# Issuing the first attention weight loads ahead of the weight-split stage, and squaring the next x tile at another place of VectorE's queue, in an attention + FFN block on eight cores

## The reference

```
xn = (x - mean) / sqrt(var + 1e-5)                    # over the 1024 features
# attention: 16 query heads, 4 kv heads, head size 64, window of 16 keys back
q = rmsnorm(xn @ wq.T); k = rmsnorm(xn @ wk.T); v = xn @ wv.T
attn = softmax(q k^T / 8 + alibi bias, masked to 0 <= i-j <= 16) @ v
a = attn @ wo.T
# FFN (RWKV channel mix); x_prev is xn shifted by one token
xr = mu_r*xn + (1-mu_r)*x_prev;  xk = mu_k*xn + (1-mu_k)*x_prev
f = sigmoid(xr @ W_r.T) * (relu(xk @ W_k.T)**2 @ W_v.T)
return x + a + f
```

## Time and profile before

| | us |
|---|---|
| median of 3 runs | 2063.03 |
| the three runs | 2060.89, 2063.03, 2120.01 |
| profiled execution, its own time | 2056.66 |
| span of its slowest core (core 5) | 2055.1 |
| spans of the eight cores | 2027.7 to 2055.1 |

### The profile page before, as it was taken

One profiled execution on the slowest core, in us unless ns is written; L12 is line 12 of the kernel. 1 busy time (PEld: TensorE's weight loads), 2 busy tenths in 40 slices (PEclk: granted clock), 3 DMA queues, 4 the chain that ended last, 5 costly groups with the idle time before them and its releaser, 6 DMA issues.

```text
span 2055.1 us, 19870 instructions; the slowest of 8 cores (2027.7 to 2055.1 us)
## 1 busy us (share of the span) xinstructions
PE 1601.4 (78%) x8032; PEld 970.7 (47%) x8032; DVE 557.7 (27%) x667; ACT 191.9 (9%) x280; POOL 273.9 (13%) x245
## 2 busy tenths in 40 slices
PE   1014987887897998789697997789699798779798
PEld 0002425885342435787242434778243343678443
DVE  1127343220013632330013723231011624332011
ACT  0000011110000011110000001110010001111010
POOL 0224400000121500000022500000022320000022
PEclk8556978986998997897899897997899897898799
DMA  7556102004214100202412210200520410200311
GB/s 208 149 161 184 41 0 82 1 1 138 68 54 136 39 17 9 74 1 75 132 41 71 94 41 0 83 1 2 163 83 21 143 41 0 82 1 1 123 57 67
DMA packets 100017, 138.14 MB, mean 67 GB/s; under 512 B 2596, under 2 KB 72488, under 8 KB 99704
## 3 DMA queue, kind: packets, MB, share of 16 engines
q1 hardware_dynamic: 96168, 121.99, 19.1%
q0 software_dynamic: 3760, 14.88, 2.1%
HBM read 115.89 MB, written 20.97 MB: 67 GB/s over the span
## 4 chain that ended last, share of the span: by engine, by line
PE 69%; DVE 9%; DMA 8%; issue 4%; ACT 4%; SPq 4%; DVEq 1%; POOL 1%; POOLq 1%; ACTq 0%
PE psA L177 33%; PE psB L177 27%; PE psS L177 8%; SPq L177 4%; DMA wslot<-hl_wr_l 2%; DVE pbuf L177 2%; DVE lrow L177 2%; DVE lbuf L177 2%; DMA qbuf<-w_wr 2%; DMA qbuf<-w_wkf 2%; DMA wslot<-w_wo 1%; ACT pbuf L177 1%; DVEq L177 1%; DVE xnbuf L177 1%; ACT ptbuf L177 1%
## 5 line engine op out<-in xcount | busy, mean ns | idle before, releaser
L177 PE MATMUL psA<-xmix,wslot 128*128 128x512 bf16 x768 | 198.3, 422 | 92.4 <-DMA wslot<-hl_wr_l 74.0
L177 PE MATMUL psA<-asub,wslot 128*128 128x112 f32 (+1 forms) x1280 | 201.0, 323 | 82.0 <-DVE xnbuf L177 35.0
L177 PEld LDWEIGHTS psA<-asub,wslot 128*128 128x128 f32 x1280 | 191.6, 237 | 87.2 <-issue 87.2
L177 PE MATMUL psA<-xnbuf,wslot 128*128 128x512 f32 x384 | 183.1, 628 | 15.6 <-DVE xnbuf L177 15.5
L177 PE MATMUL psB<-asub,wslot 128*128 128x112 f32 (+1 forms) x1280 | 187.8, 310 | 0.0
L177 PEld LDWEIGHTS psB<-asub,wslot 128*128 128x128 f32 x1280 | 181.7, 226 | 0.0
L177 PEld LDWEIGHTS psA<-xmix,wslot 128*128 128x128 bf16 x768 | 81.3, 107 | 203.3 <-issue 132.5
L177 PE MATMUL psB<-xmix,wslot 128*128 128x512 bf16 x768 | 171.0, 379 | 0.0
L177 PE MATMUL psB<-xnbuf,wslot 128*128 128x512 f32 (+1 forms) x384 | 136.0, 506 | 0.0
L177 POOL CAST xmix<-pbuf 128x512 bf16<-128x512 f32 x64 | 40.6, 634 | 678.4 <-ACT pbuf L177 573.0
L177 PEld LDWEIGHTS psA<-xnbuf,wslot 128*128 128x128 f32 x384 | 74.7, 200 | 112.1 <-issue 111.9
(11 more groups left out here) (91 smaller groups left out, 1446.4 us busy)
## 6 DMA issues: line engine op xcount, KB each, us to landing
wslot<-w_wq SPq DMA_DIRECT2D x8, 2048.0 KB, 20.5
wslot<-w_wo SPq DMA_DIRECT2D x8, 2048.0 KB, 12.6
wslot<-hl_wr_h SPq DMA_DIRECT2D x8, 1024.0 KB, 8.2
wslot<-hl_wr_l SPq DMA_DIRECT2D x8, 1024.0 KB, 9.7
wslot<-hl_wkf_h SPq DMA_DIRECT2D x8, 1024.0 KB, 10.2
wslot<-hl_wkf_l SPq DMA_DIRECT2D x8, 1024.0 KB, 19.7
wslot<-hl_wvf_h SPq DMA_DIRECT2D x8, 1024.0 KB, 5.5
wslot<-hl_wvf_l SPq DMA_DIRECT2D x8, 1024.0 KB, 8.4
```

The costliest lines, as they stand in the source:

```text
L177: inst = getattr(eng, attr)(*a, **kw)
```

## The change

1. The loads of `w_wk`, `w_wv` and both halves of `w_wq` for tile 0 are issued by SP ahead of the weight-split loop, directly behind the load of x, instead of behind the loop.
2. `load_weight_half_hl` waits for the two stores of its own half (`prep_done[(nm, half)]`) instead of for all twelve.
3. The square of x becomes `emit_x2`. In tile 0 it is called from `emit_ln_stats` as before. For later tiles it is called right behind the K phase, so that in DVE's queue it stands behind `k_evac(7)` and ahead of `v_evac(0)`, instead of between `v_evac(5)` and `v_evac(6)`. The matmuls of the statistics stay where they were.

```diff
@@ -336,7 +336,11 @@
             in_=xin3[:, :, 0:TT]), 16)
 
+        wkv_info = load_weight_half(None, 0, 0, kvpair=True)
+        wq_info = [load_weight_half(wq3, 0, 1), load_weight_half(wq3, 1, 2)]
+
         xmixbf_st = xmix.bitcast(BF16)
+        prep_done = {}
         pi = 0
@@ -366,6 +370,7 @@
                 s_po.inc(SY.dma_start(
                     out=whl3[nm][1][:, :, 512 * half:512 * half + 512],
                     in_=lo.rearrange("p (c o) -> p c o", o=512)), 16)
+                prep_done[(nm, half)] = s_po.n
                 pi += 1
@@ -376,7 +381,7 @@
                 SY.wait_ge(sem, cnt)
-            SY.wait_ge(s_po.h, PREP_PO)
+            SY.wait_ge(s_po.h, prep_done[(nm, half)])
@@ -386,8 +391,7 @@
-        wkv_info = load_weight_half(None, 0, 0, kvpair=True)
-        wq_info = [load_weight_half(wq3, 0, 1), load_weight_half(wq3, 1, 2)]
@@ -411,7 +415,7 @@
-            def emit_ln_stats(first=(tt == 0)):
+            def emit_x2(first=(tt == 0)):
                 V.wait_ge(X_READY[0], X_READY[1])
@@ -419,7 +423,12 @@
                 s_v.inc(V.tensor_tensor(scr[:, 0:NCH * TT], xbuf[:, 0:NCH * TT],
                                         xbuf[:, 0:NCH * TT], op=ALU.mult))
-                xsq = s_v.n
+                LNS["XSQ_V"] = s_v.n
+
+            def emit_ln_stats(first=(tt == 0)):
+                if first:
+                    emit_x2(first=True)
+                xsq = LNS["XSQ_V"]
                 T.wait_ge(X_READY[0], X_READY[1])
@@ -958,6 +967,8 @@
             ffn_phase_hl(wkf_info, scrbf, k_evac)
             KMM_LAST = s_t.n
+            if tt + 1 < NT:
+                emit_x2(first=False)
             wslot_free[wkf_info[0][0]] = (s_t.h, s_t.n)
```

## The result

| | before | after |
|---|---|---|
| median us | 2060.75 | 2084.16 |
| runs | 10 | 10 |
| profiled execution, its span | 2055.1 (core 5) | 2082.4 (core 4) |

The ratio after / before is 1.0111, 95% interval 1.0088 to 1.0135: 22.9 us slower (18 to 28), inside the 2% band. The forecast was + 30.0 us, within 2%.

The account below looks back on a forecast made before the run. Bound: the serial split stage up to 142 us, later PE's pace. 21.7 - 3.6 + 0 + 11.9 = + 30.0 us on 2056.66 us, plus 5.3 us for the close runs, gave 2092 us; range 2077 to 2104 us.

Parts of the forecast that it names:

- The price of the early loads: Split stage: 6.29 MB ahead of the first qbuf load delay everything behind by 21.7 us (19.1 to 26.2).
- B: Rival, split stage: the early loads don't delay the first qbuf load; + 8.3 us, 2070 us; chance 0.08.
- C: Rival, start: memory gives 190 GB/s or less to the early loads; at 183 GB/s + 42.7 us, 2105 us; chance 0.07.
- The gain at the k projection: Tile 0: the wait for w_wv goes away, gain 3.6 us, at least 0.8 us.
- Edit 2 at nothing: SP's narrower wait for stores: they have landed by then with or without it; cost 0, gain 0.
- The square hidden at its old place: V phase: the square ran beside PE's matmuls with 1.9 us to spare; moving it earlier takes nothing off PE.
- The square at its new place: K-to-V transition: the square holds POOL up, PE loses 3.95 us in each of three, + 11.9 us (7.2 to 13.5).
- a slower first group: Start of V phase: PE's first 24 matmuls slower after the longer idle time, + 0.5 us per transition (- 0.2 to + 0.9).
- Rival A: K-to-V transition: the square does not hold POOL up, only the early loads count; + 18.1 us, 2080 us; chance 0.13.
- the case that I had bounded by + 22.7 us: Whole kernel: the main case, + 30.0 us, bounds + 22.7 (2085 us) to + 38.9 us (2101 us); chance 0.68.

Follow-up runs that it names:

- e10: Only the w_wk and w_wv loads ahead of the first qbuf load, in the kernel before; ratio 0.9986 (0.9953 to 1.0020).
- e4: Kernel before with the early loads placed behind the qbuf loads of halves that POOL splits; ratio 0.9945, 11.3 us faster.
- e1: Only the four early loads ahead of the split stage, in the kernel before; ratio 1.0052, + 10.7 us (5 to 17).
- e3: As e2, but the square stands behind v_evac(0) in DVE's queue; ratio 1.0002 (0.9971 to 1.0034) against the kernel before.
- e5: As e2, but the square is cut into eight DVE instructions; ratio 0.9995 (0.9958 to 1.0032) against the kernel before.
- e6: As e2, but ACT makes the square for tiles 1 to 3; ratio 1.0005 (0.9967 to 1.0043) against the kernel before.
- e2: Only the square moved behind the K phase, in the kernel before; ratio 1.0042, + 8.6 us (3 to 14).
- e8: On top of e4, slots rotate so W_r's second half loads ahead of W_k's halves; ratio 0.9681 against the kernel before, median 1994.90 us.

## Why the prediction was right, and where it was off

**The price of the early loads: right.** 21.7 us (bounds 19.1 to 26.2) were put down. The first cast moved by 20.5 us and the square by 21.0 us as means. e10 shows that the price goes by bytes, and e4 that it is a matter of standing ahead of the first `qbuf` load. 6.29 MB in 20.5 us are 307 GB/s, and the two stretches above ran at 300 and 283 GB/s, where 290 had been taken. Rivals B (not delayed) and C (190 GB/s or less) are out.

**The gain at the k projection: mechanism right, size wrong.** This is the largest piece of what made 30 us out of 24: 2.9 us of 6.1. I read the gain, 3.6 us, off core 5 alone, and for core 5 it is right. Core 0 of the same execution shows the wait that the page of the slowest core hid, and here the trace names the DMA:

```profile
158.44 3.67 DVE L177 TENSOR_SCALAR lrow<-lrow,scal 1x528 f32<-1x528 f32 x1
...
175.20 0.70 DVE L177 TENSOR_TENSOR xnbuf<-xbuf,psS 128x528 f32<-128x528 f32 x1 [4.67 <-PE psS L177]
...
188.07 8.50 PE L177 MATMUL psA<-xnbuf,wslot 128*128 128x512 f32 x16 [12.98 <-DMA wslot<-w_wv]
```

There `xnbuf` starts 6.2 us earlier than on core 5 and the weight lands at nearly the same time, so PE waits 12.98 us. The mean distance from the start of `xnbuf` to the first copy of k was 19.0 us before (15.3 to 23.0) and is 12.6 us after, on every core: a gain of 6.5 us. Another 2.0 us came by the arrival described below, which no term of the prediction had: four cores of before reached `xnbuf` about 40 us behind the square, the others 33.5 to 34.6 us; after, one core did. 21.0 - 6.5 - 2.0 = 12.5 us, what the first copy shows, where I had 18.1 us. In e1 the time went up by 10.7 us. These are means over the cores, while the time is that of the slowest core.

**Edit 2 at nothing: right by the trace.** No run isolates it, but the traces show that there was no wait to remove. In before SP issued the last stores of the split stage at 170.5 us, they took about 10 us to land, and the first load that waits for them was issued at 236.6 us, when the q projection had freed its slot. In after these are 187.2 and 250.8 us. In neither did SP wait for a store.

**The square hidden at its old place, nothing to gain: right.** e3 has the square early and where nobody waits for POOL, and the time of before.

**The square at its new place: right.** Foreseen were a cast of about 4 us, an idle time of 7.6 us, + 3.45 us for each transition and + 0.5 us for a slower first group. Read: 4.08 us, 7.59 us, + 3.47 us, and 7.37 instead of 7.04 us as a mean, + 0.33 us. Three times 3.8 us are 11.4 us, against 11.9 us; timed alone it was 8.6 us (3 to 14). Rival A (POOL not held up) is out, and so is its reason, that a cast has one input only: the cast was held like the addition. The cast ended 0.46 us behind the square, where 0.48 us had been worked out from the addition. By an estimate from a figure of the Trainium skill, page "SBUF — State Buffer", section "A bandwidth-pool intuition that's wrong (but worth ruling out)", the end of DVE's instruction and about 115 ns, with the full cast behind it, it would have been 0.3 us later, so there the measurement decides against the estimate. The rule of the Trainium skill, same page, section "Who interferes with whom", that in such a pair whichever of DVE and POOL starts first keeps the shared ports for its whole instruction and that ACT waits for nobody, agrees with e3 (an addition of 5.45 us beside the square), e5 (a cast of 0.85 us) and e6 (0.61 us).

**Sum.** 12.5 + 11.4 = 23.9 us by the marks, 22.9 us by the time. That is the low edge of the case that I had bounded by + 22.7 us. The interval (18 to 28 us) touches rival A's + 18.1 us, so it is the marks and e2, not the time, that decide against A. The 6 us between 30.0 and 23.9 are 2.9 for the k projection's wait, 2.0 for the arrival, 0.7 for the price of the loads and 0.5 for the square; all four lie on the same side. What brought the 2.0 us isn't shown, and it may have been chance.

## What to carry to other kernels

A load moved to the front of a full DMA queue costs its transfer time for all that stands behind it; put prefetches behind the transfer that the path needs, where an engine's own work covers them. On DVE and POOL look at what the other engine does in the same microseconds: a long DVE instruction like this square, moved from slack into POOL's critical chain, costs its remaining length. Moving it by one group or giving it to ACT took the cost away, and cutting it into pieces left 0.44 us of 3.47. Read a wait on several cores before its removal is priced, and look in the page for what the engine that sets the pace waits for most: the order of the loads in SP's queue (e8) was worth 54 us, nearly five times the 11 us that the early loads brought in their best place (e4).

## What the runs showed that was not expected

In tile 0 the layer-norm rows on one partition meet POOL's last split, and a small change of arrival decides which of the two goes first: on core 0 of before the rows start 2.3 us ahead of POOL's last cast, on core 5 1.8 us. On core 0 of before the `TENSOR_SCALAR` on 1 x 528 took 3.67 us, on core 5 8.00 us; without POOL beside it, at tile 1, 0.48 us. Cores where one of these row instructions had to wait for POOL's whole subtraction (7.9 us), and not only for the rest of its cast (3.6 us), reached `xnbuf` some 6 us later. With the same queue orders this hit four of eight cores in before, three in e2, none in e3, three in e5 and none in e6. In the six kernels with early loads it hit 3 cores of 48, in these five 10 of 40; whether the early loads make it rarer isn't shown. The effect moves single cores by as much as the effects under study, so it belongs to what one must average over.

In e5 eight back-to-back DVE instructions took 6.39 us instead of 4.55 us in one piece. In tile 0, with POOL idle beside them, the eight took 5.03 us: 0.5 us is the price of the cutting, and 1.4 us are POOL's turns. POOL's cast and subtraction, 1.76 us in all when alone, took 2.21 us among them, and the longest of the eight pieces took 1.65 us where their median is 0.70 us. So both engines wait, each for the end of an instruction of the other.
